# The last block of the experts' second product contracts over 112 partitions with zeros in the first 64

## The reference, cut to what matters

```python
# x: G=8 groups of 1024 tokens, M=128 features; E=8 experts; H=688 hidden; C=256 places
expert_inputs = jnp.einsum('GSEC,GSM->EGCM', dispatch, x)
layer_w0 = jnp.einsum('EGCM,EMH->EGCH', expert_inputs, w0_kernel)
layer_w1 = jnp.einsum('EGCM,EMH->EGCH', expert_inputs, w1_kernel)
hidden = jax.nn.gelu(layer_w0, approximate=True) * layer_w1
expert_outputs = jnp.einsum('EGCH,EHM->EGCM', hidden, wo_kernel)
out = jnp.einsum('EGCM,GSEC->GSM', expert_outputs, combine)
```

## Time and profile before

| | |
|---|---|
| time, median of 3 runs | 2725.08 us (2714.4 to 2730.01) |
| time of the profiled execution | 2714.58 us |
| its span, first to last instruction | 2712.8 us |
| mean granted TensorE clock | 0.892 |
| TensorE busy (matmul, weight load) | 2122.5 us, 1580.5 us |
| VectorE, ScalarE, GpSimd busy | 1472.9, 1233.0, 645.1 us |

### The profile page before, as it was taken

How to read it: one execution, slowest core, us unless ns; L and a number is a source line. 1 busy time by engine, 2 the same in 40 slices (tenths; PEclk the granted TensorE clock), 3 DMA queues, 4 the chain that set the end, 5 groups by cost and what they waited for, 6 DMA issues and landing times.

```text
span 2712.8 us, 42689 instructions
## 1 busy us (share of the span) xinstructions
PE 2122.5 (78%) x13612; PEld 1580.5 (58%) x13612; DVE 1472.9 (54%) x4206; ACT 1233.0 (45%) x2621; POOL 645.1 (24%) x656
## 2 busy tenths in 40 slices
PE   3667572488768788998898789879988998778875
PEld 2445351366546556775686467647765775655754
DVE  5887434553465674566556565556565356346512
ACT  4766313443335445544644464445454445334421
POOL 3111003222130133123222322232233133022042
PEclk9877895699889889999999899999998999888987
DMA  7000000011211212311131113221321312311111
GB/s 234 25 0 0 1 1 0 25 35 49 61 47 39 67 46 59 80 50 52 51 87 52 44 49 87 55 59 41 79 63 53 83 54 55 81 32 52 38 56 45
DMA packets 228960, 141.40 MB, mean 52 GB/s; under 512 B 116489, under 2 KB 206732, under 8 KB 228754
## 3 DMA queue, kind: packets, MB, share of 16 engines
q1 hardware_dynamic: 174320, 85.60, 12.7%
q0 software_dynamic: 16960, 34.74, 4.5%
q10 hardware_dynamic: 37474, 18.46, 2.3%
HBM read 82.48 MB, written 57.16 MB: 51 GB/s over the span
## 4 chain that ended last, share of the span: by engine, by line
PE 51%; DVE 17%; issue 15%; ACT 9%; DMA 2%; POOL 2%; SPq 2%; another core or an unknown queue 1%; DVEq 0%; ACTq 0%; POOLq 0%
PE PS L898 14%; PE PS L866 9%; PE PS L1191 4%; PE PS L1177 4%; PE PS L1154 4%; PE PS L1172 3%; PE PS L1366 2%; DVE small L327 2%; DVE AR L1076 2%; ACT AR L1127 2%; ACT AR L827 1%; PE PS L901 1%; DVE xnT L1253 1%; PE PS L857 1%
## 5 line engine op out<-in xcount | busy, mean ns | idle before, releaser
L898 PE MATMUL PS<-AR,W 128*128 128x256 f32 x2560 | 639.7, 397 | 20.0 <-DVE AR L785 17.1
L785 DVE TENSOR_TENSOR AR<-AR,PS 128x512 f32<-128x512 f32 (+1 forms) x384 | 228.6, 597 | 666.3 <-ACT AR L827 516.3
L898 PEld LDWEIGHTS PS<-AR,W 128*128 128x128 f32 x2560 | 487.0, 199 | 90.9 <-DVE AR L785 14.0
L1127 ACT ACTIVATE AR<-PS 128x512 f32<-128x512 f32 x512 | 304.2, 599 | 376.4 <-PE PS L1177 322.3
L827 ACT ACTIVATE AR<-PS 128x512 f32<-128x512 f32 (+1 forms) x384 | 201.0, 525 | 583.6 <-PE PS L898 422.4
L1076 DVE TENSOR_REDUCE AR<-PS 128x2 f32<-128x512 f32 x512 | 339.0, 688 | 214.7 <-PE PS L1154 180.3
L866 PE MATMUL PS<-AR,WO 128*128 128x256 f32 (+1 forms) x1536 | 385.4, 393 | 0.0
L866 PEld LDWEIGHTS PS<-AR,WO 128*128 128x128 f32 (+1 forms) x1536 | 286.8, 194 | 79.8 <-issue 42.5
L1154 PE MATMUL PS<-AR 128*128 128x256 bf16 x1024 | 211.4, 295 | 55.0 <-DVE AR L1076 27.7
L1172 PE MATMUL PS<-AR 128*128 128x256 bf16 x1024 | 212.8, 292 | 52.7 <-ACT AR L1127 33.4
L1177 PE MATMUL PS<-AR,pick 96*128 96x256 bf16 x1024 | 212.3, 291 | 26.9 <-DVE AR L1089 26.6
(11 more groups left out here) (354 smaller groups left out, 2815.7 us busy)
## 6 DMA issues: line engine op xcount, KB each, us to landing
AR<-XE SPq DMA_DIRECT2D x128, 128.0 KB
YE<-AR ACTq DMA_DIRECT2D x128, 128.0 KB
AR<-QD SPq DMA_DIRECT2D x384, 32.0 KB
QD<-AR SPq DMA_DIRECT2D x8, 768.0 KB, 5.4
AR<-KD SPq DMA_DIRECT2D x64, 96.0 KB
W<-in_L_ffn_w_kernel_dram SPq DMA_DIRECT2D x2, 2560.0 KB, 13.4
OD<-AR SPq DMA_DIRECT2D x128, 36.0 KB
X<-in_L_attn_dense_dram SPq DMA_DIRECT2D x8, 512.0 KB, 4.2
```

The lines of the kernel that those rows point to most:

```text
L785: ins = dve.tensor_tensor(hf[:, cols], gl[i % 2][:, cols], H[:, 2 * (i % 2) + 1, cols], ALU.mult)
L898: mm = pe.matmul(H[:, b0, b * CAP:(b + 1) * CAP], w0[:, e, hb * P:(hb + 1) * P], xeT[e % 2], start=True, stop=True)
L1127: act.activation(EX[:, li, :], H[:, 2 + i % 2, :], ACT.Exp, scale=A_SCALE).then_inc(S["a_ex"], 1)
```

## The change

The contraction of the last block runs over partitions 0 to 111 instead of 64 to 111. The first 64 rows of that block of WO are set to zero once, in front of "consts"; the same rows of hid are set to zero once before the rounds. The number of matmuls and the columns of each stay.

```diff
         TAIL = slice(CAP, 2 * CAP)
         T0, T1 = slice(0, HLAST), slice(HALF, HALF + HLAST)
+        LASTROWS = slice(0, HALF + HLAST)
@@ second
-                    rows = slice(0, P) if b + 1 < HBLK else T1
+                    rows = slice(0, P) if b + 1 < HBLK else LASTROWS
                     mm = pe.matmul(Y[:, 0, 0:CAP], WO[rows, e, b, :], hid[e % 2][rows, b, :],
                                    start=(b == 0), stop=(b == HBLK - 1))
@@ round_pool's ones_pool
-        ONES = 4 * DEPTH + 2 * 3
+        ONES = 4 * DEPTH + 2 * 4
@@
                     ch.link(pool.memset(MP[k], 0.0))
+                    ch.link(pool.memset(hid[k][0:HALF, HBLK - 1, :], 0.0))
                 assert ch.k == ONES
@@ GpSimd's start
             ch.step(pool.memset(WT[:, :, HLAST:HALF], 0.0))
+            ch.step(pool.memset(WO[0:HALF, :, HBLK - 1, :], 0.0))
             ch.wait()
             pool.nop().then_inc(S["consts"], 1)
```

## The result

The changed kernel takes 2700.5 us in the median of six runs (2697.0 to 2708.3) where the kernel before takes 2724.3 in six (2714.4 to 2730.0): a ratio of 0.9899, 95% interval 0.9866 to 0.9932. Two more comparisons, each beside the kernel before on the same chip, gave 0.9920 (0.9896 to 0.9943) and 0.9908 (0.9876 to 0.9939). By medians it is 24, 22 and 21 us less; the forecast was 21. The ratios are not quotients of these medians; taken times the median of before they say 28, 21 and 25 us.

A forecast was written before the change was run, and what follows sets the result against it. TensorE bounds the kernel (busy 78%, 51% of the chain). Terms -17.6 - 4.3 + 0.9 = -21.0 us from the median 2725.1 give 2704.1, 0.77% less; own range 2698 to 2711, 8 in 10 range 2687 to 2720.

The forecast's parts named there:

- The gap and its cause: Experts' second product: 0.33 us idle before 48-row loads and behind them, read as layout changes; 112 rows remove it.
- My second reason: For 112-row loads acting like the gapless 96-row ones: both need the last quarter of the partitions.
- Rival (D): 112-row loads treated like 48-row ones, or shared-row loads exposed; gaps stay, about +1 us, 2726; chance 0.05.
- the rule of the Trainium skill: A weight load overlaps matmuls in flight only when its row group differs; the prediction thought the trace contradicted it.
- The size of the gap: Per expert's twelve matmuls: 0.288 us less where TensorE work follows directly, 0.194 where it waits for ScalarE's copy.
- Which passes count: 85 of 128 experts on the chain: 61 save 17.6 us, 22 stage ends 4.3, two nothing; other 43 at 0.
- the late transfer: Next attention's operands reach line 1154 no earlier; five experts' savings, 1.4 us, only lengthen TensorE's idle time there.
- The two before line 568: Two experts followed by 0.61 us idle, waiting for VectorE's line 500, which takes their saving: 0.
- The memsets: Zeros in WO before consts, uncovered: +0.9 us; two memsets of hid, covered by 5 us: 0.
- (B): All of the experts' saving is paid: 33.9 us less, 2691; chance 0.12.
- (C): A second path takes over within each stage, half the gain lost to ScalarE or VectorE waits: about -10, 2715; chance 0.13.
- (E): Slower: earlier arrival makes TensorE idle longer and lowers its granted clock; 0.02 lower gives about +20, 2745; chance 0.04.

The follow-up runs named there:

- e5: Changed kernel with the last block's rows varied by expert (32 to 112 rows, starting at partition 0, 32 or 64), product partly left out; one run, 2707.6 us.
- e3: Changed kernel with 112 rows for 93 experts only; 35 (0, 1, 3 to 7 of the second mixture, 16-expert stages) keep 48; 2618.8 us, ratio 0.9912.
- e4: Changed kernel with the matmul edit undone (48 rows again) and both memsets kept; 2636.6 us against 2640.9 before, ratio 0.9994.
- e1: Changed kernel again, no edit, on a second chip; 2618.8 us against 2640.9 before, ratio 0.9920.
- e6: Changed kernel once more, no edit; 2702.3 us against 2723.8 before, ratio 0.9908.
- e7: Changed kernel with a second buffer for the result that ScalarE copies out and the zeros of WO written later; 2699.1 us, ratio to before 0.9916.
- e2: Changed kernel with 112 rows only for 35 experts (0, 1, 3 to 7 of the second mixture, 16-expert stages), others 48; 2632.7 us, ratio 0.9982.
- e8: Changed kernel with the zeros of WO written later and line 1139's 24-row contraction widened to 128 rows; 2692.2 us, ratio to before 0.9879.

## Why the prediction held, step by step

**The gap and its cause: right.** The loads before and behind the last block no longer wait, the shape reads 112 rows, and the mean went from 428 to 379 ns. I had put 112 rows with 96 and not with 48 by nearness alone; e5 turns that into a line between 64 and 80 rows. (My second reason was wrong in part: 96 rows from partition 0 end at 95 and leave the last quarter free.) That the gap is a change of the array's layout is my reading; the traces show the gap and what it depends on. Rival (D) falls, and with it the rule of the Trainium skill ("TensorE: Matmul & The Clock Gate", Part 3, "The mechanism") that the prediction quotes: e5's loads of 80 to 112 rows, over partitions that the matmul in flight uses too, wait 0.8 us in 32. The prediction also drew a wrong consequence from that rule. Partitions 64 to 111 lie within the 128 that the matmul in flight uses, so these are no rows apart from it, and the rule did not clearly make the 48-row block the cheap one.

**The size of the gap: too small.** I took 0.288 us for each pass in which TensorE runs on: the distance to the start of the next matmul. The change back costs a little more behind that. Two passes near the end, when nothing but the experts runs, before:

```profile
2657.42 2.95 PE L866 MATMUL PS<-AR,WO 128*128 128x256 f32 x12
2660.30 0.44 PE L857 MATMUL PS<-ident,AR 128*128 128x128 f32 x2
2660.57 3.62 PE L898 MATMUL PS<-AR,W 128*128 128x256 f32 x16
2665.55 2.73 PE L866 MATMUL PS<-AR,WO 128*128 128x256 f32 x11
```

After:

```profile
2652.16 2.76 PE L867 MATMUL PS<-AR,WO 128*128 128x256 f32 x12
2654.75 0.38 PE L858 MATMUL PS<-ident,AR 128*128 128x128 f32 x2
2654.97 3.62 PE L899 MATMUL PS<-AR,W 128*128 128x256 f32 x16
2659.94 2.76 PE L867 MATMUL PS<-AR,WO 128*128 128x256 f32 x12
```

From pass to pass it is 8.13 and 7.78; unrounded 8.124 and 7.783, 0.341 less. The missing 0.05 lies in the two transposes behind: 60.57 - 60.30 = 0.27 us until line 898 may start, 0.22 after. Measured over a whole period instead of to the next start, the term is 61 x 0.341 = 20.8, and the sum -20.8 - 4.3 + 0.9 = -24.2 instead of -21.0. Six such passes and two ends make 6 x 0.341 + 2 x 0.194 = 2.43 us for a second half: the 2.4 that three of the five show.

**Which passes count: right in the main, with the wrong reason for half of it.** In the first half of a middle stage the savings bring next to nothing, in the second half all of theirs, 2.4 us; and e3, without the 35, has the gain of the whole change. The prediction said that the late transfer would take what the five experts in front of it save (3 to 7), and gave no reason for the others. But 1.16 us of each such half go into the four waits for ScalarE and VectorE, behind experts 0, 1, 3 and 7, and only what 4, 5 and 6 save is left for the transfer to take. The two before line 568 gave nothing, as forecast: in after TensorE waits 0.81 us there, for line 500 of VectorE, where it had waited 0.61. Of the other off-chain experts, 19 were never tested by themselves. Nor is the chain a property of the kernel alone: counted in the same way it holds the last two matmuls of 85 experts in before and of 83 in e4, which has the same matmuls, and of 74 in after and 73 in e1 and e6. So it is likely that not each of the 85 counted in full.

**The memsets: right.** 0.94 us in front of consts, line 2563 at 16.91 instead of 16.03, no cover. Those of hid take 0.30 us each in after; the last ends at 454.4, and VectorE is busy with its own work until 458.8, so they delay nobody.

**The rivals.** (B), that all of it is paid: 33.9 us by my figures, a ratio of 0.9876. The first interval (from 0.9866) alone would still hold that; e1's (from 0.9896) does not, and with 0.341 it would be 39.5 us, 0.9855, outside all three. It falls. (C), a second path: its sign, longer waits for line 809 (810 of after), is there in the first halves, as shown; it took what I had already counted at 0. In the second halves none takes over. The stores into YE are there without the change and cost nothing measurable (e7). (E), the clock: it scatters but not in one direction. The attention behind one stage, the same work, by the table by stretch in e4:

```profile
1680.00:1790.00 110.00, 87.41 (x820) 59.67 (x821) 70.24 (x197) 61.25 (x118) 37.88 (x38) 0.94 0.22 60
```

And in e1:

```profile
1672.00:1784.00 112.00, 91.09 (x820) 61.00 (x821) 70.49 (x197) 61.26 (x118) 37.62 (x38) 0.89 0.22 59
```

e1 had its matmuls busy 3.7 us longer for the same 820, at a clock of 0.89 instead of 0.94. e3, with the same change in the stage ahead, had 0.94 there. So this is one stage of one execution, a few us; before and after have 0.92 and 0.93 over all that follows 540 us.

**What stays open.** With 0.341 the sum is 24.2 and the three medians give 24, 22 and 21; the width of each comparison, 0.5 to 0.7% of 2700 us, does not tell whether a few us are lost again to longer waits or slices of slow clock. One such wait is TensorE's longest in the last stage, 6.19 us before line 876 in before and 10.63 in after. One trace of each says little of such a wait; on the second chip it is 8.74 and 8.58 (before line 858) where the experts of that stage are unchanged (e4, e2) and 9.42 and 9.49 where they are changed (e3, e1). Some 0.8 us may be lost there. That the forecast of 21 meets the medians to within 3 us is in part luck: the pass was priced 3.2 us too low over the 61, and the 85 were all counted in full.

## What to carry to other kernels

Look in the groups by shape for a form with idle time before its weight loads that is put down to "issue" and is the same for each: a matmul over 64 rows or fewer in a stream of full ones cost more here than a full one, and zeros in its unused rows were cheaper. Price such a gap over a whole period of the loop, not to the next instruction. Then count only the places where the chain of waits passes through it, and look behind each place for a wait on another engine: the savings in the first half of a middle stage were worth next to nothing here, and equal ones in the second half 2.4 us. The chain of one profile is a good guide to that and not an exact one.

## What the runs showed of the hardware that I had not expected

- The line lies between 64 and 80 rows and the start partition doesn't matter: 32, 48 and 64 rows wait 0.33 us before each pair of loads, 80, 96 and 112 wait 0.8 us in 32 loads (e5).
- A 24-row group of 16 small matmuls costs 0.20 us in the same way with bf16 operands, and 128-row loads for matmuls of eight columns come as fast, one in 0.033 us (e8).
- The kernel before took 2724 us in the median in the first and third comparison and 2641 in the second, on another chip, 3% apart, while the ratio of after to before was 0.990, 0.991 and 0.992. A time from another chip says nothing about a change of 1%; the runs beside it do.
